# Split-float32 attention: six bf16 products in 96 rows become three float32r products in 48, two heads in the row halves of TensorE

## The reference, cut to what matters

```
q = _apply_rope(proj(WQ_w, WQ_b), cos, sin);  k = _apply_rope(proj(WK_w, WK_b), cos, sin)
scores = einsum('bhqd,bhkd->bhqk', q, k) / sqrt(16)
scores = where(causal, scores, -inf);  attn = softmax(scores, -1)
out = einsum('bhqk,bhkd->bhqd', attn, v)

qp = einsum('bld,ed->ble', q, Wq);  idx = argmax(qp @ kv^T, -1)
mk, mv = split(kv[idx] @ Wkv^T)
out = softmax(einsum('bhld,bmd->bhlm', qh, mk) / sqrt(16), -1) @ mv
```

## Time and profile before

| | |
|---|---|
| runs | 1334.55, 1334.60, 1335.56 us, median 1334.6 |
| profiled execution: first to last instruction (no other time of it was kept) | 1332.9 us |
| TensorE busy | 1165.2 us, 87% (6681 matmuls) |
| VectorE busy | 976.3 us, 73% |
| ScalarE busy | 624.5 us, 47% |
| GpSimd busy | 183.0 us, 14% |
| mean granted clock of TensorE | 0.917 of full speed |

### The profile page before, as it was taken

The page is one execution under the profiler, slowest core; times in us unless marked ns, Lnnn a source line. Parts: engine busy times, 40 slices in busy tenths (PEclk is TensorE's granted clock), DMA queues, the critical chain, the costliest instruction groups (busy, mean ns, idle before and its releaser), DMA issues. The chain is left out here.

```text
span 1332.9 us, 18064 instructions
## 1 busy us (share of the span) xinstructions
PE 1165.2 (87%) x6681; PEld 626.0 (47%) x6681; DVE 976.3 (73%) x2195; ACT 624.5 (47%) x838; POOL 183.0 (14%) x165
## 2 busy tenths in 40 slices
PE   6854999999999999964999389999986799999997
PEld 3521233333333333243788112333335489898997
DVE  4474999898899988145799489999918466767675
ACT  1320245756756666841443015666653334444442
POOL 2223111021021100153000430500004000000000
PEclk9785799999999999986999559999987899999999
DMA  6215066920000000030110583200011000000000
GB/s 241 83 60 101 24 69 78 111 30 1 2 2 1 1 1 1 1 132 28 48 48 1 61 98 44 84 1 2 1 50 56 1 1 1 16 1 17 1 16 17
DMA packets 43928, 51.19 MB, mean 38 GB/s; under 512 B 7002, under 2 KB 39258, under 8 KB 43834
## 3 DMA queue, kind: packets, MB, share of 16 engines
q1 hardware_dynamic: 43834, 49.97, 19.2%
HBM read 37.83 MB, written 11.53 MB: 37 GB/s over the span
## 5 line engine op out<-in xcount | busy, mean ns | idle before, releaser
L583 ACT ACTIVATE self_probs<-self_scores 128x1024 f32<-128x1024 f32 (+3 forms) x320 | 273.3, 894 | 199.7 <-PE self_scores L537 198.3
L611 DVE TENSOR_REDUCE self_piece_max<-self_max 128x1 f32<-128x512 f32 x384 | 249.9, 685 | 24.2 <-PE self_max L522 22.8
L522 PE MATMUL self_max<-stack_k,stack_q 96*128 96x512 bf16 (+3 forms) x640 | 209.7, 368 | 21.2 <-DVE self_piece_max L611 8.7
L611 DVE TENSOR_REDUCE cross_piece_max<-cross_max 128x1 f32<-128x512 f32 x256 | 160.6, 683 | 25.2 <-PE cross_max L522 24.5
L583 ACT ACTIVATE cross_probs<-cross_scores 128x1024 f32<-128x1024 f32 x128 | 124.6, 1021 | 108.9 <-PE cross_scores L537 108.8
L537 PE MATMUL self_scores<-stack_q,stack_k 98*128 98x512 bf16 (+3 forms) x640 | 170.7, 351 | 4.3 <-DMA stack_q<-self_shift 3.0
L522 PEld LDWEIGHTS self_max<-stack_k,stack_q 96*128 96x128 bf16 x640 | 61.9, 98 | 202.8 <-DVE self_piece_max L611 104.3
L548 PE MATMUL self_out<-self_probs,V 128*17 128x512 f32 (+3 forms) x1280 | 149.7, 540 | 2.4 <-ACT self_probs L583 2.1
L607 DVE CUSTOM_DVE_ANT_0 self_junk<-self_max,causal_sb 128x128 bf16<-128x128 f32 (+3 forms) x256 | 120.8, 484 | 21.3 <-PE self_max L522 19.8
L1270 ACT ACTIVATE o_tok<-ph 128x512 f32<-128x512 f32 x96 | 57.5, 599 | 143.7 <-PE ph L92 137.5
L92 PE MATMUL py<-w_first,hid_first 128*128 128x256 f32 x384 | 108.7, 283 | 5.7 <-DVE x_sb L1332 5.7
(11 more groups left out here) (209 smaller groups left out, 1772.1 us busy)
## 6 DMA issues: line engine op xcount, KB each, us to landing
stack_q<-qparts SPq DMA_DIRECT2D x96, 64.0 KB, 8.6
stackx<-xparts SPq DMA_DIRECT2D x24, 256.0 KB, 10.9
stack_k<-kparts SPq DMA_DIRECT2D x18, 256.0 KB, 14.3
qparts<-parts SPq DMA_DIRECT2D x8, 384.0 KB, 2.5
kparts<-parts SPq DMA_DIRECT2D x8, 384.0 KB, 2.5
xparts<-xparts_sb SPq DMA_DIRECT2D x8, 384.0 KB, 2.7
cross_raw<-in_w SPq DMA_DIRECT2D x4, 768.0 KB, 4.9
n_raw<-in_w SPq DMA_DIRECT2D x6, 512.0 KB, 4.4
```

What stands on the lines that cost most here:

```text
L522: mm = nc.tensor.matmul(slot[:, 0:pc["w"]], pc["lhsT"], pc["rhs"], start=True, stop=True)
L583: nc.scalar.activation(probs[:, i % 3, 2 * pair:2 * pair + 2, st["off"]:C], ps[:, 2 * pair:2 * pair + 2, st["off"]:C], ACT.Exp, scale=SCAL ...
L611: ins = nc.vector.tensor_reduce(to, slot[:, 0:pc["w"]], AX.X, ALU.max)
```

## The change

- `PAIRS` has three products of two float32r parts: 48 rows of 4 bytes in place of 96 of 2. The queries, keys and context keys are written to DRAM in two parts; the second cast and the third part go.
- Two heads share a stack: one in partitions 0 to 63, one in 64 to 127 (`ROWS` = 2, `HALF` = 64). The pieces and the score matmuls alternate between the halves. Their number and their columns stay.
- The causal mask of the maximum is added by TensorE: two bf16 matmuls of 128 columns over 64 rows after the piece, into the same bank. All pieces are then reduced by L607, a plain reduction.
- ScalarE copies a unit's output out of PSUM, after the exponentials of the next unit's first step. The mark goes: the shift itself frees the buffer.
- The rows of ones come by DMA, not from GpSimd. The shifts of a unit are four transfers.
- For the few keys, the parts are added first, then split by two ScalarE copies and a VectorE subtraction.

The core of the diff:

```diff
-PAIRS = [(0, 0), (0, 1), (1, 0), (0, 2), (2, 0), (1, 1)]
+PAIRS = [(0, 0), (0, 1), (1, 0)]
+ROWS = 2
+HALF = P // ROWS
...
-                            pool.wait_ge(p2_ready, n + 1)
-                            if n:
-                                pool.wait_ge(p3_ready, n)
-                            nc.gpsimd.tensor_tensor(parts[:, n % 2, 2], rest[:, n % 2], parts[:, n % 2, 1], ALU.subtract).then_inc(p3_ready, 1)
+                            pool.wait_ge(p1_ready, n + 1)
+                            nc.gpsimd.tensor_tensor(parts[:, n % 2, 1], whole[:, n % 2], parts[:, n % 2, 0].bitcast(F32),
+                                                    ALU.subtract).then_inc(p2_ready, 1)
...
-                            act.wait_ge(rest_ready, n + 1)
-                            nc.scalar.copy(parts[:, n % 2, 1], rest[:, n % 2]).then_inc(p2_ready, 1)
...
-                            nc.vector.tensor_tensor(rest[:, n % 2], whole[:, n % 2], parts[:, n % 2, 0], ALU.subtract).then_inc(rest_ready, 1)
...
-                                for b, dst in enumerate(work["shift_to"]):
-                                    sp.dma_start(dst, shift[:, u % 2, b]).then_inc(shift_in[u % 2], 16)
+                                for h in range(ROWS):
+                                    for b in range(2):
+                                        rows = slice(h * UR // ROWS, (h + 1) * UR // ROWS)
+                                        sp.dma_start(work["shift_to"](h, b).bitcast(F32), shift[rows, u % 2, b].bitcast(F32)).then_inc(shift_in[u % 2], 16)
...
-                                    mm = nc.tensor.matmul(slot[:, 0:pc["w"]], pc["lhsT"], pc["rhs"], start=True, stop=True)
+                                    mm = nc.tensor.matmul(slot[:, 0:pc["w"]], pc["lhsT"], pc["rhs"], start=True, stop=not pc["diag"])
+                                    if pc["diag"]:
+                                        own = slice(pc["half"] * HALF, (pc["half"] + 1) * HALF)
+                                        for r in range(ROWS):
+                                            mm = nc.tensor.matmul(slot[:, pc["w"] - P:pc["w"]], mask_at[own, r], mask_of[own, r],
+                                                                  start=False, stop=r == ROWS - 1)
...
+                        def output_copy(steps, i):
+                            u = steps[i]["unit"]
+                            act.wait_ge(probs_used, i + 1)
+                            if u >= 2:
+                                act.wait_ge(inverse_ready, u - 1)
+                            nc.scalar.copy(acc_sb[:, u % 2], po[:]).then_inc(acc_copied, 1)
...
-                        for j in range(GH):
+                        for z in range(GH // ROWS):
                             for n, a in enumerate(range(0, end, C)):
                                 b = min(a + C, end)
-                                pieces.append(dict(w=b - a, lhsT=stack_q[g][0:KS, c, j, q * P:(q + 1) * P],
...
+                                for h in range(ROWS):
+                                    own = slice(h * HALF, h * HALF + KS)
+                                    pieces.append(dict(w=b - a, lhsT=stack_q[g][own, c, z, q * P:(q + 1) * P], rhs=stack_k[g][own, z, a:b],
...
-                            keys=lambda j, g=g, kt=kt: stack_k[g][0:KS + 2, j, kt * P:(kt + 1) * P],
+                            keys=lambda j, g=g, kt=kt: stack_k[g][j % ROWS * HALF:j % ROWS * HALF + KS + 2, j // ROWS, kt * P:(kt + 1) * P],
```

More of the change, by code:

```diff
@@ L62, in decoder_layer @@
 def decoder_layer(nc, x, xT, ctxT, wq, bq, wk, bk, wv, bv, wo, bo, xwq, xwkv, xwc, rw, w1, w2,
-                  cosT, sinT, identity, below, causal, iota, out):
+                  cosT, sinT, identity, below, masks, iota, out):
     top = ExitStack()
@@ L585, in program @@
                                                          scale=SCALE).then_inc(probs_ready, 1)
+                                if i and steps[i - 1]["last"]:
+                                    output_copy(steps, i - 1)
+                            output_copy(steps, len(steps) - 1)
+                        def output_copy(steps, i):
[4 more added lines that the diff above has]
+                            nc.scalar.copy(acc_sb[:, u % 2], po[:]).then_inc(acc_copied, 1)
                         either(act, program)
@@ L638, in program @@
                             for i in range(len(thirds)):
-                                for item in thirds[i][0] + thirds[i][1]:
-                                    side_item(item)
-                                if 1 <= i <= len(steps) and steps[i - 1]["last"]:
-                                    u = steps[i - 1]["unit"]
-                                    dve.wait_ge(probs_used, i)
-                                    nc.vector.tensor_copy(acc_sb[:, u % 2], po[:]).then_inc(acc_copied, 1)
-                                for item in thirds[i][2]:
+                                for item in thirds[i][0] + thirds[i][1] + thirds[i][2]:
                                     side_item(item)
@@ L1021, in _ @@
                                     split(i)
-                                for i in ahead[n]:
-                                    split_rest(i)
                                 for a, b in cols:
@@ L1360 @@
     below = (rows[:, None] < rows[None, :]).astype(np.float32)
-    tri = np.where(np.arange(P)[None, :] > rows[:, None], np.float32(MASKED), np.float32(0.0))
-    causal = np.concatenate([np.zeros((P, C - P), np.float32), tri], 1)
+    own = HALF * np.arange(ROWS)[None, :] + (rows % HALF)[:, None]
+    masks = np.stack([(rows == own[:, :, None]).astype(np.float32),
+                      np.where(rows > own[:, :, None], np.float32(MASKED), np.float32(0.0))])
     data = dict(
```

283 lines of the change are left out of this document (132 added, 151 removed).

## The result

The changed kernel is slower. The median of its first four runs is 1356.8 us (1344.1 to 1373.0) against 1334.7 us before; ratio 1.014, 95% interval 1.012 to 1.017. Run again it took 1355.1 to 1363.4 us, ratio 1.019 (1.016 to 1.023). The forecast was 1281 us.

| stage | before, us | after, us | difference |
|---|---|---|---|
| projections, to the first load of the self-attention | 105.3 | 98.0 | -7.3 |
| from there to the first scores | 20.4 | 23.2 | +2.8 |
| self-attention, steps 0 to 19 | 90.1 | 116.9 | **+26.8** |
| self-attention, steps 20 to 139 | 319.5 | 320.7 | +1.2 |
| its tail | 41.9 | 47.2 | +5.3 |

The account below looks back on a forecast made before the run. TensorE was taken to bound full steps (2.81 us), with VectorE right behind (2.48). The terms -37.5 - 14.6 - 7 + 4 + 2.4 - 0.5 = -53 us took 1334.6 to 1281 us, range 1262 to 1312.

Parts of the forecast that it names:

- Masked reduction and copy off VectorE: Both attentions: VectorE loses 13 output copies in each, 8.9 and 9.0 us; the masked reduction becoming plain gains nothing.
- The price of a pair: Score matmuls in two row halves: a pair costs 0.25 us, between bounds of 0.227 and 0.454.
- The rival that the halves don't overlap: Score matmuls and pieces: the row halves don't run side by side, so the kernel gets slower, 1384 us; chance 7%.
- Masks: Mask matmuls of 128 columns on TensorE: 0.08 us each, 480 of them 38 us, bounds 0.055 and 0.11 each.
- So TensorE falls to or under VectorE's 2.48: Full attention step: TensorE's work falls from 2.81 to 2.48 us, or 2.07 with pieces in pairs, against VectorE's 2.48.
- VectorE plus 12.7 us: Self-attention steps: VectorE's 359.3 us of work plus 12.7 us left above it, 372 for 409.5, so -37.5 us.
- The clock: Rival for both attentions: a TensorE waiting for VectorE falls to half clock more often, 1334 us, no change; chance 5%.
- Projections: Projection stage: a subtraction and a cast go per unit, against more transfers; -7 us, bounds -3 and -10.
- starts: Starts of the two attentions: more transfers in the first load and in a unit's shifts, together +4 us.
- Tails: Tails of the two attentions: ScalarE is the bound and two output copies in each stand in the way, +2.4 us.
- The cross-attention: Cross-attention steps: VectorE's 167.2 us of work plus 5.3, 172.5 for 187.1, so -14.6 us; bounds 0 and -20.
- the likeliest case: Whole kernel: the forecast itself, 1281 us, its own range 1262 to 1297; chance 68%.

## Why the prediction was wrong

Point by point, by its own steps:

- **Masked reduction and copy off VectorE**: right. 358.7 and 166.5 us of work are left, forecast 359.3 and 167.2.
- **The price of a pair**: right. 0.23 us from pair to pair, 0.35 for the one whose weights wait (taken: 0.25). The rival that the halves don't overlap is out.
- **Masks**: mis-sized, without weight. 0.105 each instead of 0.08, close to the upper bound of 0.11 that the earlier trace rows gave, and mostly in TensorE's wait.
- **"So TensorE falls to or under VectorE's 2.48"**: the first step that failed. TensorE's own work did fall under it (the eighth matmul could start at 441.16), but a full step is 2.69, and the sum of 372 us for the stage became 437.6. The working set the two engines' sums side by side and took the larger. It never followed one buffer round: piece, values, next piece, reduction. In the kernel before the values came 0.30 us after their piece and took 0.99, and the next reduction began at 424.94, 0.42 after its piece; with the same 0.74 for the release that loop was 2.45 us, hidden under TensorE's 2.82. Float32r made both exposed ends of it longer: the values come 0.42 us after the piece instead of 0.30, and the reduction 0.53 after its piece instead of 0.42, of which 0.08 each are the weight load of a piece that has waited, 0.18 us rather than 0.10. In place of "VectorE plus 12.7 us" VectorE stood still for 79 us.
- **The clock**: the second step that failed. Its rival had the mechanism in the wrong place (a TensorE that waits) and 5 in 100. Its measure against it, "TensorE still has some 2.3 us of work in a step", is no measure: the clock was low with TensorE busy 98% of the time. What had changed were the rows in use, 98 to 50 a matmul, which stands in the list of the change and which the prediction priced at nothing without a reason. The runs with fewer products show that fewer rows bring the clock down in either kernel (0.92 to 0.71, and 0.88 to 0.71); whether float32r adds to it in the changed kernel stays open. It cost 26.8 us in steps 0 to 19, and part of the +5.3 in the tail, where the clock was 0.84.
- **Projections** -7.3 (forecast -7) and **starts** +5.1 (forecast +4): right in size; no run took them apart. **Tails** +5.1 for +2.4, **between** -2.6 for -0.5.
- **The cross-attention** gave -5.6 of -14.6. It has the same loop (2.69 us), and unit-end steps of 3.87 us that were 3.65.

So the likeliest case failed with -52 forecast for both attentions and +22 measured: some 27 of these 74 us are the clock at the start, some 37 to 39 are the self-attention's steady gain that did not come (the loop accounts for 0.2 us of each full step; the steps with narrow pieces, which grew, were not taken apart), 9 the cross-attention's. At the clock of before the change would by this be worth 1356 - 27 = some 1329 us, 0.4% (an estimate, not run). The one part that gains is the copy on ScalarE, and it gains more in the old kernel (1324.0 us, the best version found) than the whole change.

## What to carry to other kernels

Where two engines pass buffers to each other, the busy sums are only lower bounds: follow one buffer round, with the start-up of every instruction that waits for it, and count how many pieces there are to a buffer; a faster engine gives nothing once this loop is the longest. And a change that makes matmuls use fewer rows of the array, at the same number and columns, can keep the clock low for longer: look for it first, and read the granted clock of the first 100 us of such a stage rather than the mean. Try the parts of a change alone; here one part was worth 9 us and the rest cost some 30.

## What the runs showed of the hardware

- TensorE's clock went with the rows in use: mean 0.92, 0.84 (in one execution 0.90) and 0.71 of full speed with 96, 64 and 32 rows of data in otherwise equal bf16 matmuls, and with 32 rows 0.51 over 308 us in which TensorE was never idle. Two halves of 32 rows side by side gave 0.71 too, two of 48 rows in float32r 0.86 to 0.90. Why, whether rows of zeros count, and what float32r does to it, stays open; so does why executions with 64 rows differed.
- Matmuls of zeros over all 128 rows brought the clock up within 10 us and it fell back soon after the attention's own matmuls began, in both kernels.
- VectorE's maximum of 128 x 512 from PSUM follows at 0.60 us when pieces are always ready.
- Two row halves start within 0.01 us of each other and cost one matmul's 0.23 us; one matmul over all 128 rows between them started 0.09 us late and took 0.42 us of the stream, where alone they follow at 0.22.
